# Gated linear attention and a post-norm FFN: the layer-norm scalars and the gate product of a tile are issued on GpSimd instead of VectorE

## The reference

```
for each sequence x [4096, 1024]:
    q, k = heads(x@Wq)/16, heads(x@Wk); v = heads(x@Wv)          # 4 heads, dk 256, dv 512
    gk = log_sigmoid(x@gk_w1@gk_w2 + gk_b2) / 16
    S_t = S_{t-1} * exp(gk_t) + k_t v_t^T;  o_t = q_t S_t         # scan over time
    g  = x@Wg
    o  = o * rsqrt(mean(o*o) + 1e-5) * g_norm_w * (g*sigmoid(g))
    y  = layernorm(x + o@Wo)
    yp = y shifted by one position
    r  = sigmoid((mu_r*y + (1-mu_r)*yp) @ W_r^T)
    ka = square(relu((mu_k*y + (1-mu_k)*yp) @ W_k^T))
    out = layernorm(y + r * (ka @ W_v^T))
```

## Time and profile before

| | us |
|---|---|
| median of the runs shown (2) | 2402.69 |
| the two runs | 2333.7 and 2471.68 |
| the profiled execution, its own time | 2335.31 |
| its span (slowest core, core 3) | 2333.7 |
| spans of the 8 cores | 2308.4 to 2333.7 |

### The profile page before, as it was taken

One profiled execution on the slowest core, in us unless ns is written; L12 is line 12 of the kernel. 1 busy time (PEld: TensorE's weight loads), 2 busy tenths in 40 slices (PEclk: granted clock), 3 DMA queues, 4 the chain that ended last, 5 costly groups with the idle time before them and its releaser, 6 DMA issues.

```text
span 2333.7 us, 31040 instructions; the slowest of 8 cores (2308.4 to 2333.7 us)
## 1 busy us (share of the span) xinstructions
PE 1730.9 (74%) x11392; PEld 1086.1 (47%) x11392; DVE 1313.7 (56%) x2837; ACT 477.8 (20%) x563; POOL 48.1 (2%) x65
## 2 busy tenths in 40 slices
PE   0388888888888888883776786887763777787775
PEld 0155555555555555552444554454442444444442
DVE  0144444454444444443566666665665478877776
ACT  0123333223233323331110101001001121122210
POOL 0000000000000000000000000000000000000000
PEclk9999999999999999997898898777987899989998
DMA  7885441110111111004542423323312211111120
GB/s 96 104 100 100 64 64 28 28 24 14 28 28 28 28 28 27 20 19 108 172 109 64 120 70 99 91 64 100 91 68 96 103 59 66 62 73 73 73 73 37
DMA packets 128840, 157.34 MB, mean 67 GB/s; under 512 B 4321, under 2 KB 102626, under 8 KB 128242
## 3 DMA queue, kind: packets, MB, share of 16 engines
q0 software_dynamic: 42784, 56.76, 15.7%
q1 hardware_dynamic: 85906, 98.59, 13.0%
HBM read 144.98 MB, written 65.01 MB: 90 GB/s over the span
## 4 chain that ended last, share of the span: by engine, by line
PE 55%; DVE 27%; issue 7%; DMA 7%; ACT 3%; DVEq 1%; ACTq 0%; SPq 0%; POOLq 0%
PE PO L601 9%; PE PBIG L569 7%; PE PBIG L320 7%; PE PBIG L353 5%; PE PBIG L763 5%; PE PO L369 5%; PE PO L751 4%; PE PO L466 3%; DVE F L335 3%; PE PBIG L448 2%; PE PO L473 2%; DVE F L620 2%; DVE F L626 2%; DVE B L769 2%; PE PBIG L420 2%
## 5 line engine op out<-in xcount | busy, mean ns | idle before, releaser
L569 PE MATMUL PBIG<-B,arena 128*128 128x256 bf16 x2048 | 275.3, 305 | 161.8 <-ACT F L576 122.3
L569 PEld LDWEIGHTS PBIG<-B,arena 128*128 128x128 bf16 x2048 | 222.3, 109 | 215.5 <-issue 166.9
L601 PE MATMUL PO<-arena,O 128*128 128x512 bf16 x1024 | 241.1, 395 | 25.1 <-DVE F L609 23.9
L576 ACT ACTIVATE F<-PBIG 128x1024 f32<-128x1024 f32 x64 | 65.5, 1024 | 571.9 <-DVE Y L672 444.2
L327 DVE CAST V<-PBIG 128x512 bf16<-128x512 f32 x128 | 86.6, 687 | 167.9 <-PE PBIG L320 164.3
L601 PEld LDWEIGHTS PO<-arena,O 128*128 128x128 bf16 x1024 | 98.9, 100 | 161.3 <-issue 87.9
L580 DVE TENSOR_SCALAR V<-F,gnw_s 128x256 bf16<-128x256 f32 x256 | 73.4, 350 | 159.2 <-ACT F L576 159.2
L614 DVE SCALAR_TENSOR_TENSOR F<-PO,rstdA,F 128x1024 f32<-128x1024 f32 x96 | 123.3, 1284 | 53.2 <-PE PO L601 51.1
L320 PE MATMUL PBIG<-arena,B 128*128 128x512 bf16 x512 | 130.8, 423 | 10.8 <-ACT F L311 10.8
L320 PE MATMUL PBIG<-arena,B1u 128*128 128x512 bf16 x512 | 130.6, 423 | 9.8 <-ACT F L311 9.8
L751 PE MATMUL PO<-arena,B 128*128 128x512 bf16 x256 | 62.9, 405 | 64.8 <-DMA arena<-wktbf 39.8
(11 more groups left out here) (130 smaller groups left out, 2611.8 us busy)
## 6 DMA issues: line engine op xcount, KB each, us to landing
orms<-O SPq DMA_DIRECT2D x16, 1024.0 KB
X<-x SPq DMA_DIRECT2D x16, 1024.0 KB
O<-orms SPq DMA_DIRECT2D x16, 1024.0 KB
ybuf<-Y SPq DMA_DIRECT2D x16, 1024.0 KB
Y<-ybuf POOLq DMA_DIRECT2D x16, 1024.0 KB, 5.3
out<-X SPq DMA_DIRECT2D x16, 1024.0 KB
B<-xt POOLq DMA_DIRECT2D x24, 512.0 KB, 8.9
arena<-wv POOLq DMA_DIRECT2D x1, 4096.0 KB, 30.0
```

The lines of the kernel that those rows point to most:

```text
L569: fns.append(lambda E, m=m, mm=mm, kc=kc, b0=b0, xfm=xfm: E.matmul(PBIG[:, b0 * 512 + mm * 256:b0 * 512 + (mm + 1) * 256], arena[:, A2_WG ...
L601: fns.append(lambda E, tb=tb, ng=ng, kc=kc, kk=kk, p=po: E.matmul(p[:, ng * 512:(ng + 1) * 512], ot[:, kc * 256 + tb * 128:kc * 256 + tb * ...
```

## The change

A sixth name, `pool`, is added to the scheduler. Its groups go into the queue of `gpsimd`, in order with that queue's DMA issues, but count on a semaphore of their own, and in the paranoid build they wait for earlier `pool` groups on the same buffer. A `gpsimd` DMA does not wait for `pool` groups. Two kinds of groups get this name: the product of o and the gate (L588 of before, 2 for each tile of A2), and all 21 small instructions of `emit_ln_tail` (in A2 and B). The two wide instructions at the end of the tail (L672) stay on VectorE. The arithmetic and the order of emission are unchanged.

```diff
-ENGS = ("tensor", "vector", "scalar", "gpsimd", "sync")
+ENGS = ("tensor", "vector", "scalar", "gpsimd", "sync", "pool")
@@ need
         if peng == eng:
-            if not (self.paranoid and eng in ("vector", "scalar")):
+            if not (self.paranoid and eng in ("vector", "scalar", "pool")):
                 return
+        if peng == "pool" and eng == "gpsimd":
+            return
...
-        self.q[eng].append(lambda E, p=peng, v=val: E.wait_ge(self.sem[p], v))
+        self.q["gpsimd" if eng == "pool" else eng].append(
+            lambda E, p=peng, v=val: E.wait_ge(self.sem[p], v))
@@ group
+        phys = "gpsimd" if eng == "pool" else eng
...
-            self.q[eng].append(fn)
+            self.q[phys].append(fn)
@@ emit_a2_tile
-                    S.group("vector", [lambda E, o=ot, kh=kh: E.tensor_tensor(
+                    S.group("pool", [lambda E, o=ot, kh=kh: E.tensor_tensor(
                         o[:, kh * 2048:(kh + 1) * 2048],
                         o[:, kh * 2048:(kh + 1) * 2048],
                         V1t[:, kh * 2048:(kh + 1) * 2048], ALU.mult)],
@@ emit_ln_tail (5 groups of sums, 4 of the first guess, 3 x 4 of Newton)
-            S.group("vector", [lambda E: E.tensor_scalar(
+            S.group("pool", [lambda E: E.tensor_scalar(
                 statr[:, 4:6], statr[:, 0:2], inv, None, ALU.mult)], writes=[bSTAT])
...
-                S.group("vector", [fn], writes=[bSTAT])
+                S.group("pool", [fn], writes=[bSTAT])
...
-                    S.group("vector", [fn], writes=[bSTAT])
+                    S.group("pool", [fn], writes=[bSTAT])
```

More of the change, by code:

```diff
@@ L65, in group @@
                 self.need(eng, u)
+        phys = "gpsimd" if eng == "pool" else eng
         n = 16 if dma else 1
         if dma and self.cnt[eng]:
-            self.q[eng].append(
+            self.q[phys].append(
                 lambda E, e=eng, v=self.cnt[eng]: E.wait_ge(self.sem[e], v))
         for fn in fns[:-1]:
-            self.q[eng].append(fn)
+            self.q[phys].append(fn)
         self.cnt[eng] += n
@@ L76, in last @@
             fn(E).then_inc(self.sem[e], k)
-        self.q[eng].append(last)
+        self.q[phys].append(last)
         tok = (eng, val)
@@ L191, in build_program @@
         s_sy = ES.enter_context(nc.semaphore("s_sy"))
+        s_pl = ES.enter_context(nc.semaphore("s_pl"))
         block = ES.enter_context(nc.Block())
@@ L195, in build_program @@
         sems = {"tensor": s_te, "vector": s_ve, "scalar": s_se,
-                "gpsimd": s_gp, "sync": s_sy}
+                "gpsimd": s_gp, "sync": s_sy, "pool": s_pl}
         S.sem = sems
@@ L639, in emit_ln_tail @@
             inv = float(1.0 / D)
-            S.group("vector", [lambda E: E.tensor_scalar(
+            S.group("pool", [lambda E: E.tensor_scalar(
                 statr[:, 4:6], statr[:, 0:2], inv, None, ALU.mult)], writes=[bSTAT])
-            S.group("vector", [lambda E: E.tensor_scalar(
+            S.group("pool", [lambda E: E.tensor_scalar(
                 statr[:, 6:8], statr[:, 2:4], inv, None, ALU.mult)], writes=[bSTAT])
-            S.group("vector", [lambda E: E.tensor_tensor(
+            S.group("pool", [lambda E: E.tensor_tensor(
                 statr[:, 8:10], statr[:, 4:6], statr[:, 4:6], ALU.mult)], writes=[bSTAT])
-            S.group("vector", [lambda E: E.tensor_tensor(
+            S.group("pool", [lambda E: E.tensor_tensor(
                 statr[:, 10:12], statr[:, 6:8], statr[:, 8:10], ALU.subtract)], writes=[bSTAT])
-            S.group("vector", [lambda E: E.tensor_scalar(
+            S.group("pool", [lambda E: E.tensor_scalar(
                 statr[:, 24:26], statr[:, 4:6], -1.0, None, ALU.mult)], writes=[bSTAT])
```

## The result

The changed kernel takes 2521.59 us (median of 11 runs), the kernel before, run beside it, 2337.59 (10 runs). The ratio is 1.0801 with a 95% interval of 1.0758 to 1.0844: 8% slower. Some executions of both kernels take 4 to 6% longer, with a lower granted clock on one half of the chip; the medians include them, the ratio leaves them out. The profiled execution has a span of 2505.4 us against 2333.7, so the traces account for 171.7 us.

The account below looks back on a forecast made before the run. Neither TensorE nor VectorE is full; the handover between them, with the tail's latency on A2's path, sets the pace. 41 + 4 + 78 + 15 + 34 + 14 = 186 us on 2333.7 gives 2520 us, range 2400 to 2660.

Parts of the forecast that it names:

- A2, tail's steps: Tail in A2: 21 steps at 0.40 us on GpSimd, 8.40 us against 5.86, 16 tails, 41 us.
- A2, second product: Gate product for kh = 1 in A2: 4.58 us on GpSimd, TensorE waits 2.11 us more per tile, 34 us.
- A2, clock: Matmuls after A2's product wait: half the tiles lose 1.7 us at a lower clock, 14 us, bounds 0 and 27.
- B, with its last two tiles: Pass B: late load of Y 78 us, its meeting with the store 15, slower tails in the last two tiles 4.
- The load of Y: Pass B: queued behind the tail on GpSimd, it starts the transposes 5.6 us late in 14 tiles, 78 us.
- the meeting: Pass B: the late load of Y overlaps the store of X, 1.1 us in each of 14 tiles, 15 us.
- The load of transposed x: A2: also moved behind a tail, but its data are wanted a tile later, some 25 us left; no cost.
- the load would be hidden: Rival for B: the late load of Y is hidden, B pays 26 us instead of 93; 2453 us, chance 0.12.
- the product would be as fast as VectorE's: Rival for A2's gate product: -20 us instead of 34, no fall of the clock; 2452 us, chance 0.08.
- steps would be dear: Rival for the tail: each GpSimd step takes 0.69 us, paying the DMA issue's wake-up; 2715 us, chance 0.13.
- it would not be slower: Rival for the tail: GpSimd chains small steps more cheaply, 0.13 us each; 2339 us, chance 0.04.
- The lock between the engines: Rival in A2: VectorE's L609 must wait for GpSimd's product, 22 us more; 2542 us, chance 0.07.

Follow-up runs that it names:

- e4: Kernel before, all on VectorE, with one wait added: the load of Y also waits for the tail's last small step; ratio 1.0297.
- e9: Kernel before, with A2's SiLU written to a separate place for each quarter in the scan's state instead of F1; ratio 0.9542.
- e7b: Kernel before with only the first gate product of a tile (kh = 0) on GpSimd; no ratio, span 2318.3 us.
- e6b: Kernel before with only the second gate product of a tile (kh = 1) on GpSimd; ratio 1.0171.
- e3: Changed kernel with the load of Y put ahead of the tail in GpSimd's queue, the 21 steps still on GpSimd; ratio 1.0529.
- e8b: Changed kernel with A2's load of transposed x put ahead of the tail in GpSimd's queue; ratio 1.0781.
- e1: Changed kernel with the tail's 21 steps put back on VectorE, only the two gate products on GpSimd; ratio 1.0174.
- e2: Changed kernel with the gate products put back on VectorE, only the tail's 21 steps on GpSimd; ratio 1.0497.
- e10: Changed kernel with A2's SiLU written to a separate place for each quarter instead of F1; 2417.6 us, ratio 1.0418.

## Why the prediction was right

The forecast was 2520 us, slower, by 186 us of span; 171.7 were measured in the traces, and 2521.59 is the median. That the medians agree to 2 us is partly luck: the sum was added to a span, and the spans differ by 14 us less than forecast. The terms differ too, and against e4, the cleaner reference for A2, by more:

| term | forecast | measured against the trace of before | against e4's A2 |
|---|---|---|---|
| A2, tail's steps | 41 | 33 (wait for SiLU, 122.3 to 155.2) | 27.5 |
| A2, second product | 34 | 33 (wait, 23.9 to 57.1) | 29.4 |
| A2, clock | 14 | 16 (matmuls, 516.4 to 532.5) | 36.7 |
| B, with its last two tiles | 97 | 88 (517.5 to 605.6) | |

- **What bounds it.** Right. e9 shows that the tail's price in A2 is the wait through F1, and e7b and e6b that a product costs only where TensorE waits for it.
- **The steps.** 0.347 us each, where I took 0.40 between 0.20 and 0.69. That makes the tail 7.29 us in A2, not 8.40, and 23 us instead of 41. L677's extra 0.35 us in 11 tiles (4 us) and a start 0.05 us later in each make it the 27.5 against e4.
- **The load of Y.** Right, and shown both ways by e3 and e4. In the tile shown the transposes were 6.35 us late (16.87 less 10.52); forecast were 5.6 and 1.1 for the meeting. The tile of B was forecast as 37 us and is 37.3. The issue came behind the last step, the load took 1.42 us longer and not 1.1, and the shorter tail made up for it.
- **The load of transposed x: put at nothing.** Its data came in time, as forecast, but its issue falls on L677, a cost that was not thought of: e8b, which moves it away, has an A2 9.9 us shorter.
- **The product.** 4.05 us, forecast 4.58 from two passes at the slowest row's pace. TensorE's wait grew by 1.79 in the tile shown, forecast 2.11, and by 29.4 us over e4's in all, forecast 34.
- **The clock: under-sized.** I let half of the tiles lose 1.7 us behind the product, with bounds of 0 and 27 us. In the trace all 16 show 12.3 us or more for the 48 matmuls, where ten of before had 10.61, and 11 of them 13.1 to 13.5, more than the 12.29 that I had taken for the worst; the projection is 35.9 us longer than e4's, outside the bounds. The gate matmuls behind the tail changed little, as forecast (265.4 us against e4's 264.6). e1, with the same wait of 3.48 us, is mixed, as its rows show:

```profile
1381.45 9.99 PE L574 MATMUL PBIG<-B,arena 128*128 128x256 bf16 x64 [8.42 <-ACT F L581]
1398.37 13.55 PE L606 MATMUL PO<-arena,O 128*128 128x512 bf16 x48 [3.48 <-POOL O L593]
...
1427.68 9.09 PE L574 MATMUL PBIG<-B,arena 128*128 128x256 bf16 x64 [8.77 <-ACT F L581]
1443.70 10.61 PE L606 MATMUL PO<-arena,O 128*128 128x512 bf16 x48 [3.48 <-POOL O L593]
```

So the two edits do not add up. Over e4's A2, e1 costs 36.7 us, e2 24.1, both together 93.8. Of the 33.0 left over, 31.1 are matmul time (projection 35.9 - 15.0 + 3.0, gate 0.8 + 4.0 + 2.4). The longer wait at the tail and the longer wait at the product make each other dearer by the clock. Why the clock fell in every tile of the changed kernel and in some of e1 was not settled; the waits at the product are equal in both. The trace of before held some 21 us of matmul time at a lower clock, which hides most of this in the comparison with it.

- **The rivals.** That the load would be hidden (2453 us), that the product would be as fast as VectorE's (2452), that steps would be dear (2715) and that it would not be slower (2339) are out. The lock between the engines was priced at one place only, and it is not there: L614 (L609 of before), which reads PSUM, takes 1.28 us beside the product, as without it. It does occur at L677 and L585, as below.

## What to carry to other kernels

Before moving small dependent steps to an idle engine, ask what waits for the last of them: the time of an engine that has nothing else to do meanwhile is worth nothing, and each step's handover comes with it. Count what the new engine already has in its queue and what is issued behind: here a DMA issue that had run ahead of the tail cost more by standing behind it (67 us in e4) than all 21 steps by being slower (24 us in A2 of e2, 9 in B of e3). What paid was to free the buffer that made others wait for the tail, and then to write the tail in fewer steps.

## What the runs showed of the hardware

GpSimd's dependent steps on 128x2 columns cost 0.347 us start to start (0.18 to 0.22 busy), VectorE's 0.279; by the median tile 0.344 and 0.270. Its product of 2048 bf16 columns takes 4.05 us when nothing disturbs it, 3.3 times VectorE's 1226 ns.

The two engines do hold each other up, in both directions. A tile of the changed kernel in which the DMA issue came late:

```profile
1402.70 1.53 DVE L677 TENSOR_SCALAR Y<-F,statr 128x1024 f32<-128x1024 f32 x2 [7.38 <-POOL statr L672]
1403.42 1.31 POOL L525 DMA_DIRECT2D B<-xt  x1 [0.83 <-issue]
...
1409.18 4.05 POOL L593 TENSOR_TENSOR O<-O,V 128x2048 bf16<-128x2048 bf16 x1 [4.45 <-DVE V L585]
1411.80 2.36 DVE L585 TENSOR_SCALAR V<-F,gnw_s 128x256 bf16<-128x256 f32 x4 [2.84 <-ACT F L581]
...
1416.63 1.28 DVE L614 TENSOR_SCALAR F<-PO,rstdA 128x1024 f32<-128x1024 f32 x1
1416.67 4.05 POOL L593 TENSOR_TENSOR O<-O,V 128x2048 bf16<-128x2048 bf16 x1 [3.44 <-DVE V L585]
```

L677 is two instructions, 0.73 us apart. In 11 tiles of A2, as in the one shown first, the issue comes 0.43 us after the first starts; the second then takes 1.15 us instead of 0.81, and the pair 1.88. In this tile the issue comes with the second one: the pair keeps its 1.53 us and the issue takes 1.31 us instead of 0.96. The four L585, 1.14 us elsewhere, take 2.36 when they start inside a product, and the delay is all in the first of them: it starts at 1411.80 and ends at 1413.38, 0.15 us after the product, having taken 1.57 us instead of 0.35. In e10, where L589 comes first, its instructions keep their pace and the product takes up to 5.80 us. L614, from PSUM, is untouched. The Trainium skill (SBUF — State Buffer, section Who interferes with whom) says that tensor_scalar can enter a mode that takes the port pair shared with GpSimd, and that the one that starts first keeps it; the trace agrees for these SBUF-to-SBUF instructions and the product. For the DMA issue, which in both tiles starts while the first half of L677 runs, the order of start alone does not say who gives way. The prediction had looked at L609 only, and left out L580 and L672, which read SBUF.
